# Five unread matmuls behind the sums of squares of eleven layer norms

## What is computed

```python
def _layernorm(x, axis=-1, eps=1e-05):
    m = jnp.mean(x, axis=axis, keepdims=True)
    v = jnp.var(x, axis=axis, keepdims=True)
    return (x - m) / jnp.sqrt(v + eps)
...
xn = _layernorm(x, axis=-1)
x = x + _L0_gnn_ref(xn, ...) + _L0_mix_ref(xn[None], ...)[0]
x = x + _L0_ffn_ref(_layernorm(x, axis=-1)[None], ...)[0]
...
```

## Time and profile before

| | |
|---|---|
| median of 3 runs | 5286.51 us (5283.10 to 5288.95) |
| time of the profiled execution | 5281.22 us |
| its span, first to last instruction | 5279.4 us |
| TensorE busy | 4878.1 us (92%) |
| VectorE, ScalarE busy | 1026.3 us, 1011.0 us (19% each) |
| mean granted TensorE clock | 0.968 of full |

### The profile page before, as it was taken

The page is one execution under the profiler, slowest core; times in us unless marked ns, Lnnn a source line. Parts: engine busy times, 40 slices in busy tenths (PEclk is TensorE's granted clock), DMA queues, the critical chain, the costliest instruction groups (busy, mean ns, idle before and its releaser), DMA issues.

```text
span 5279.4 us, 41695 instructions
## 1 busy us (share of the span) xinstructions
PE 4878.1 (92%) x16012; PEld 2327.2 (44%) x16030; DVE 1026.3 (19%) x1998; ACT 1011.0 (19%) x1736; POOL 29.6 (1%) x55
## 2 busy tenths in 40 slices
PE   8999999999999999988999999998899988888887
PEld 6444444444445545444444444444534433333333
DVE  3771111213101316012200000102721000000000
ACT  0121112232103326122201010102511111111111
POOL 0000000000000000000000000000000000000000
PEclk9999999999999999999999999898999999999999
DMA  2012222121231110103111212231034399999998
GB/s 111 1 68 81 69 69 76 58 66 48 89 95 56 52 60 1 56 20 104 56 60 59 75 44 90 77 100 52 9 104 150 147 409 412 413 408 413 413 417 369
DMA packets 111651, 720.40 MB, mean 136 GB/s; under 512 B 13120, under 2 KB 13312, under 8 KB 72624
## 3 DMA queue, kind: packets, MB, share of 16 engines
q1 hardware_dynamic: 107568, 689.09, 34.8%
q10 hardware_dynamic: 2016, 18.49, 0.9%
q0 software_dynamic: 1952, 11.18, 0.6%
HBM read 711.90 MB, written 6.82 MB: 136 GB/s over the span
## 4 chain that ended last, share of the span: by engine, by line
PE 81%; DMA 11%; DVE 4%; ACT 2%; issue 1%; SPq 0%; ACTq 0%; DVEq 0%
PE bank L353 75%; DMA mem<-in_experts 11%; PE bank L507 3%; PE bank L474 2%; PE bank L351 1%; DVE rstd L1556 1%; DVE mem L1813 1%; ACT mem L1266 0%; DVE mem L1795 0%; ACT mem L1000 0%; DVE mem L1791 0%; DMA mem<-in_edges 0%; DVE mem L1559 0%; ACT mem L1142 0%; DVE mem L1553 0%
## 5 line engine op out<-in xcount | busy, mean ns | idle before, releaser
L353 PE MATMUL bank<-mem 128*128 128x512 f32 (+6 forms) x11616 | 3953.2, 569 | 241.5 <-DMA mem<-in_experts 126.8
L353 PEld LDWEIGHTS bank<-mem 128*128 128x128 f32 (+3 forms) x11616 | 1721.6, 173 | 2434.5 <-issue 2306.6
L1000 ACT ACTIVATE mem<-bank,cols 128x512 f32<-128x512 f32 (+1 forms) x139 | 95.8, 689 | 976.2 <-PE bank L353 976.2
L1000 ACT ACTIVATE mem<-bank 128x512 f32<-128x512 f32 x174 | 104.0, 598 | 579.6 <-PE bank L353 563.8
L507 PE MATMUL bank<-mem 128*128 128x512 bf16 x798 | 177.8, 382 | 1.2 <-DVE mem L1642 0.3
L2037 DVE TENSOR_TENSOR mem<-mem,EV 128x512 f32<-128x512 f32 x48 | 33.2, 692 | 669.4 <-ACT EV L1512 669.4
L1566 DVE TENSOR_TENSOR mem<-mem,EV 128x512 f32<-128x512 f32 x48 | 33.2, 693 | 642.0 <-ACT EV L1011 642.0
L353 PE MATMUL bank<-mem,ones 128*128 128x512 f32 (+1 forms) x232 | 109.8, 646 | 25.8 <-ACT mem L1034 17.4
L507 PEld LDWEIGHTS bank<-mem 128*128 128x128 bf16 x816 | 79.9, 98 | 99.2 <-issue 3.8
L1791 DVE SCALAR_TENSOR_TENSOR mem<-mem 128x2048 f32<-128x2048 f32 x27 | 61.8, 2290 | 300.2 <-ACT mem L1266 300.1
L474 PE MATMUL bank<-mem 128*128 (+1 forms) x544 | 117.9, 379 | 1.2 <-ACT rstd L1037 0.8
(11 more groups left out here) (287 smaller groups left out, 2301.4 us busy)
## 6 DMA issues: line engine op xcount, KB each, us to landing
mem<-in_experts SPq DMA_DIRECT2D x282, 1536.0 KB, 12.8
mem<-in_weights SPq DMA_DIRECT2D x462, 512.0 KB, 3.6
mem<-in_experts ACTq DMA_DIRECT2D x6, 1536.0 KB, 14.7
mem<-in_feats ACTq DMA_DIRECT2D x3, 2048.0 KB, 22.1
scratch<-mem POOLq DMA_DIRECT2D x5, 1024.0 KB, 4.9
mem<-scratch POOLq DMA_DIRECT2D x5, 1024.0 KB, 7.2
mem<-in_feats ACTq DMA_DIRECT2D x1, 2560.0 KB, 34.9
mem<-in_xT SPq DMA_DIRECT2D x1, 1536.0 KB, 6.7
```

Of the source, the lines that this page charges most:

```text
L353: ins = nc.tensor.matmul(out, lhsT, rhs, start=start, stop=stop)
L1000: nc.scalar.activation(dst(m), src[0:width, :], func, scale=scale, **how).then_inc(bank_free.sem, bank_free.tick((label, m)))
```

## The change

FILL = 5 is added. In norm_sums, behind the six matmuls of the squares and their release, TensorE issues five more matmuls of ones by the square chunks 0 to 4 into bank 5, for every norm but ln0. Nothing reads bank 5 there, nothing waits for them, and they wait for nothing. Each opens its own sum. All else stays.

```diff
@@ -43,6 +43,7 @@
 SHIFT = EC // 2 * P // 2
 AHEAD = 12
+FILL = 5
 ROUND = 1.5 * 2 ** 23
@@ -432,6 +433,9 @@
                     pe.wait_ge(act_done.sem, act_done.at((label, "sq", k)))
                     ins = mm(bank[6][:, :], ones[:, :], sq[:, k, :], k == 0, k == KC - 1, k == KC - 1)
                 ins.then_inc(agg_done.sem, agg_done.tick((label, "var")))
+
+                for k in range(FILL if label != "ln0" else 0):
+                    mm(bank[5][:, :], ones[:, :], sq[:, k, :])
```

## The result

The changed kernel took 5250.44 us (median of 6 runs, 5248.25 to 5263.48), the one before 5286.74 us on the same chip (6 runs, 5283.10 to 5288.95): a ratio of 0.9939, 95% interval 0.9926 to 0.9952. (The ratio is worked out over all executions and is not the quotient of the two medians; by it the gain is 32 us.) The profiled execution took 5248.76 us, 32.5 us less than the profiled one before.

What follows compares the result with a forecast made beforehand. TensorE, busy 92% of the span, was taken to bound the kernel; -25.84 us at ten gaps plus 4.28 at lny made -21.56, so 5286.51 would become 5264.9 us, range 5257 to 5276.

Steps and rivals of the forecast that it cites:

- The gaps: At ten waits behind norms, added matmuls are hidden and the clock holds; first twelve instructions take 5.42 us, gaining 25.84 us.
- only the short gaps hold: Rival, chance 0.11: the clock still falls at the three lnh gaps, 8.45 us stay, gain 13.1 us, 5273.4 us.
- the wait of 1.45 us: Ahead of the squares in an lnh, the clock stayed 1.00; nearest case for holding with 0.7 or 1.6 us idle.
- lny: Behind lny's squares nothing covers the ten added instructions, so rgat starts later and the cost is 4.28 us.
- The step that called that the whole effect: Behind lny, VectorE is no buffer, so the 4.28 us arrive in full and are not absorbed later.
- The rest of the kernel: Outside the ten gaps and lny, the sum counted no change in time.
- another draw of the phases: Rival without its own chance: unequal excess behind gaps gives 11.6 to 25.4 us; two norms' slow squares add 3.4 either way.
- The last stage: From the first expert matmul to the end: begins earlier by TensorE's gain, keeps its length, near 1099 us.
- The clock doesn't follow: Rival, chance 0.08: all ten stretches behind the gaps stay as long, only lny's price remains, 5290.8 us.
- added matmuls at half clock: Rival, chance 0.04: the ten instructions behind the squares take 8.55 us and overrun the gaps; +15.6 us, 5302.1, slower.

Runs made afterwards that it cites:

- two delayed kernels: The kernel before with one or with two unread matmuls (0.86 and 1.71 us) ahead of the loop gnn0: 5285.68 us and 5284.10 us.
- changed, delay 1: The changed kernel with one unread matmul (0.86 us) ahead of the loop gnn0: 5251.51 us (5245.58 to 5263.83), ratio 0.9930.

## Why the prediction was wrong in size

**The gaps: right.** Full clock behind all ten (of the squares ahead, ln2's alone were still slow), waits of 0.7 and 1.6 us left, first twelve at 5.3 to 5.42 us, 25.9 us against 25.84. The case that only the short gaps hold did not come; the wait of 1.45 us was a good enough neighbour. With FILL = 3, larger rests held too, mostly.

**lny: the price right, the rest not.** The ten instructions take 4.28 us and nothing hides them. The step that called that the whole effect failed: alone, they cost 11 us, because the stage behind moved against the clock's steps and took 10.6 us more, of which the stages up to ln7 gave 2.8 back.

**The rest of the kernel: the step that failed.** The sum let every stage outside the ten gaps keep its time, and the case *another draw of the phases* bounded them at two norms' squares, 3.4 us. Four squares, the router, a place in the attention and smaller ones gave some 15 us in the profiled execution, of which the last stage took 3.9 back; and rgat alone can cost 10.6 to 12.8 us more. The rows to see it were there: rows 6 showed the slow squares, and the page's mean clock, 0.968, leaves about 340 us at half clock, of which the ten stretches were only about 53. The forecast costed 53 of 340 and held the rest still, while moving the program by 20 us. Some 100 us at half clock went, twice what it had counted.

**The chance of such a draw was seen as scatter of the result; it is a systematic change.** Before, the ten slow stretches held the program in one alignment with the clock: in the profiles of before and of its two delayed kernels, and, to judge by the small scatter, in the other executions. It was one in which five norms' squares and the router were slow, yet rgat was cheap. The change took away what it was meant to, and with it the lock. What an execution now gets depends on where it starts against the clock's steps, and there are two bunches some 15 us apart. The segments of *changed, delay 1* (5263.83 us) and *changed* (5248.76) differ by rgat's price and by squares. Both profiles of the changed kernel itself are from the lower bunch, so that its upper bunch has the same cause is argued and not shown. That the upper bunch lies inside the predicted range is luck: no term of the sum put it there.

**The last stage.** From the first expert matmul on it took 1103.4 us where it was to stay near 1099, 3.9 us more than before. Nine of the thirteen other profiles have +1.1 to +4.1 us from ln7's reciprocal to the end, the two delayed ones of before +2.2 and +2.6: the profile before was a favourable draw there, and that may be a part of the 5.3 us by which the median stood above it.

**The rivals.** *The clock doesn't follow* and *added matmuls at half clock* are refuted by the first twelve at 5.42 us behind the gaps and by 9.71 us for 22 instructions. What the Trainium skill says (TensorE: Matmul & The Clock Gate, "Part 1: The HAM clock gate") of steps that run free of the program is what the delays show here, and it deserved more weight than I gave it.

## What to carry to other kernels

Filling a wait of TensorE with unread matmuls is worth the slow stretch behind it, here 2.6 us for each of ten, if the filler ends before the wait does and little idleness is left. Where TensorE goes on without a wait the filler costs its own time, and what leaving it out brings must be measured: here it moved the stage behind. When a change moves the program against the clock, add up the time at half clock in the whole trace, not only at the edit: all of it may change. And look at the single executions: one alignment or several shows there, and a median of five or six can land in either bunch (5250.4 and 5265.7 us for the same kernel).

## What the runs showed of the hardware

A stretch at half clock behind a wait ends at a place in time that the program does not set, and so it halves a delay (0.70 us against the clock's steps at the first lnh, 0.34 and 0.16 at the next two). One stage of 555 us with the same instructions took up to 12.8 us more, with VectorE and ScalarE unchanged to 0.4 us, by where it began against the clock's steps: 85.3 us of it at half clock instead of 61.4. The clock can fall in a long row of small matmuls without a wait, too: 48 router instructions of 8 columns took 7.87 us in one alignment and 5.42 in another. Matmuls whose result nobody reads keep the clock up: the same twelve instructions behind ln6's gap took 7.91 us without five of them ahead and 5.42 with them.
